# A windowed-attention block: other PSUM banks, another order of steps, and channels dealt over the partitions so that turned rows travel in single transfers

## The chip, the core and the metric

The kernel runs on one core of a Trainium2 chip. The core has a matrix engine (TensorE, PE in the profile; its weight loads are PEld), a vector engine (DVE), a scalar engine (ACT), a general engine (POOL) and an engine that issues DMA transfers (SP). They run side by side and meet at semaphores. The metric is the device time of one execution in microseconds; less is better.

## What is computed

A shifted-window transformer block over an image batch x of 4 x 256 x 256 x 96 in fp32: windows of 8 x 8 tokens, three heads of 32 channels, and an MLP of 384.

```
xs = roll(x, (-4, -4)); win = windows of 8x8 tokens of xs     # (n, 64, 96)
h = layernorm(win) * g1 + b1
q, k, v = h @ wq + bq, h @ wk + bk, h @ wv + bv               # 3 heads x 32
attn = softmax(q @ k.T / sqrt(32)); o = attn @ v
win = win + o @ wo + bo
h2 = layernorm(win) * g2 + b2
win = win + gelu(h2 @ w1 + b1) @ w2 + b2
out = roll(windows back to image, (4, 4))
```

## The kernel before, in words

**Units and batches.** A unit is half a row of windows: 16 windows, 1024 tokens, in an SBUF tile `stream` of 128 partitions x 8 tiles x 96 channels. There are 256 units in 16 batches. A batch first runs 16 attention steps, then the MLP of its 16 units. The order on each engine is written out by hand; engines wait for each other through counting semaphores.

**An attention step** works on three units at once: `back` = u, `middle` = u + 1, `front` = u + 2. PE does the scores of middle (L641), three transposes of the probabilities of back (L655), two of four q/k projections of front (L608), attention times v of back (L670), the other two projections, the v projection of front in two halves (L625), and the output projection of back in two halves (L684). DVE takes maxima of the scores (L1012), subtracts them (L1019), sums the exponentials (L1027), inverts the sums (L1035), adds the output projection into `stream` (L1041, twice) and takes statistics (L958). ACT copies out of PSUM (L806 transposed probabilities, L796/L800 q and k, L823 the attention output oT, L811 v), does the exponentials (L817) and copies the upper part of the turned, normalised input of the unit after front, `hT_upper` (L788, two halves). POOL scales the probabilities by the inverse sums (L385, three operations), makes `hT_lower` = whole minus upper (L393, two halves), and carries the arithmetic of the layer norms (L406 to L434, with the power at L425). PSUM has eight banks, and a matmul that reuses a bank has to wait until the former content has been copied out. The first half of v and the second half of the output projection share bank 6, so the second L684 waits for ACT's copy of v.

**Turned rows.** The projections want channels on the partitions. DVE transposes blocks of 32 x 32 (L1005 for the first layer norm, h1; L1072 for the second, h2), SP sends the result to a DRAM scratch tensor and fetches it back in the other order. For h2 that is three transfers of 4 x 32 x 256 elements out (L282) and one of 96 x 1024 back (L288). For h1 it is one of 128 x 3 x 256 out (L300) and three of 32 x 4 x 256 back (L310). In the MLP stretch `raw_late` (the tiles `h_raw_odd` and `oT`) takes the fetched h2 rows.

**An MLP unit.** PE runs three matmuls for each of three chunks of w1 in two parts (L718, `up`), ACT the gelus (L860), PE the second product (L732, `down`), DVE adds into `stream` (L1041). Three units ahead DVE normalises and turns (L1055, L1062, L1072), SP sends and fetches, ACT copies the upper part (L869), DVE and POOL make the lower part (L1079, L475). POOL adds b2 (L482), and does statistics for two units in the odd steps and for four units at once in steps 2 and 6. ACT also normalises the next batch's units (L777, `normalise1`, eight operations), DVE turns them. SP interleaves sends, fetches and the stores of finished units (L276: two transfers for a left half, six for a right half).

**What sets the order.** Each engine and SP's queue work in program order. A wait at the head holds all that stands behind it.

## Time and profile before

| | |
|---|---|
| median of three runs | 5499.32 us (5499.07 to 5499.84) |
| profiled execution | 5499.27 us, of which the span from first to last instruction is 5495.1 us |
| busy share of the span | PE 88%, PEld 73%, DVE 73%, ACT 72%, POOL 69% |
| mean granted TensorE clock | 0.976 of full speed |
| DMA | 622.24 MB, 113 GB/s over the span; 37.9% of 16 engines |

A busy share is a mean over stretches of different kind, so it says little alone. The profile's other views are: sums of waits (who waited for whom), a timeline for an engine (start, length, line, output and inputs, and in brackets the idle time before it and what ended it), and busy time by windows.

### The profile page before, as it was taken

How to read it: one execution, taken by the hardware profiler on the slowest of the kernel's cores; microseconds unless marked ns; L12 is line 12 of the kernel's file. 1: busy time of each engine (PE TensorE's matmuls, PEld its weight loads, DVE VectorE, ACT ScalarE, POOL GpSimd, SP SyncE). 2: the span in 40 equal slices, each digit the busy share in tenths (PEclk: the TensorE clock that was granted, in tenths of full speed). 3: DMA queues.
4: the chain of work that ended last, by engine and by line, in shares of the span. 5: the costliest groups of instructions: out<-in, count | busy, mean ns of one | idle time of the engine just before them, and what ended most of it. 6: DMA issues, size and time to landing. Idle time of an engine off the chain costs nothing.

```text
span 5495.1 us, 291417 instructions
## 1 busy us (share of the span) xinstructions
PE 4849.6 (88%) x109308; PEld 4009.3 (73%) x109308; DVE 4037.0 (73%) x9010; ACT 3956.6 (72%) x8309; POOL 3805.3 (69%) x4329
## 2 busy tenths in 40 slices
PE   6898889899898888988989888898988989888888
PEld 4777777777777777777777777777777777777777
DVE  7868768687686876868767687776877768677686
ACT  6877667686676767768677686776867677676776
POOL 6767757677575876757767577675776757767576
PEclk9999999999999999999999999999999999999999
DMA  4353433434334243343433434234342343523334
GB/s 122 112 149 95 121 104 96 145 90 122 104 99 139 89 131 102 104 132 93 133 93 112 127 92 141 87 111 126 91 144 88 114 121 89 151 88 115 112 93 148
DMA packets 443044, 622.24 MB, mean 113 GB/s; under 512 B 46009, under 2 KB 352538, under 8 KB 442586
## 3 DMA queue, kind: packets, MB, share of 16 engines
q1 hardware_dynamic: 441024, 617.92, 37.9%
q14 instruction: 449, 3.68, 0.2%
q10 hardware_dynamic: 1562, 0.50, 0.0%
q8 instruction: 9, 0.15, 0.0%
HBM read 309.96 MB, written 308.28 MB: 113 GB/s over the span
## 4 chain that ended last, share of the span: by engine, by line
PE 23%; DVE 20%; issue 17%; ACT 17%; DMA 9%; SPq 6%; POOL 5%; ACTq 2%; DVEq 1%; POOLq 0%
PE psum L732 8%; DVE row_max L1012 5%; DMA turned_rows<-probs 4%; PE psum L684 4%; ACT hT_upper L788 4%; DVE stats L958 3%; SPq L276 3%; PE psum L718 3%; DMA oT<-turned_rows 3%; PE psum L655 3%; POOL rstd L425 2%; DVE probs L1019 2%; DVE normed L1055 2%; PE psum L608 2%; PE psum L641 2%
## 5 line engine op out<-in xcount | busy, mean ns | idle before, releaser
L385 POOL TENSOR_TENSOR probs<-probs,prob_inv 128x512 f32<-128x512 f32 x771 | 782.7, 1044 | 1042.0 <-DVE prob_inv L1035 1042.0
L1041 DVE TENSOR_TENSOR stream<-stream,psum 128x384 f32 (+1 forms) x1024 | 551.3, 549 | 783.9 <-PE psum L684 484.8
L777 ACT ACTIVATE normed<-stream,shift,rstd 128x96 f32 (+1 forms) x2176 | 809.4, 462 | 76.5 <-POOL shift L434 43.0
L806 ACT ACTIVATE gelu_odd<-psum 128x512 f32<-128x512 f32 x768 | 403.5, 597 | 553.5 <-PE psum L655 553.4
L425 POOL TENSOR_TENSOR rstd<-variance,minus_half 128x16 f32<-128x16 f32 (+2 forms) x249 | 781.5, 3138 | 20.2
L684 PE MATMUL psum<-wo_w,oT 128*64 128x96 f32 x8192 | 460.4, 256 | 337.4 <-ACT v L811 337.2
L958 DVE BATCH_NORM_STATS2 stats<-stream 128x6 f32 (+2 forms) x4224 | 716.8, 243 | 42.2 <-DVE stream L1041 20.4
L684 PEld LDWEIGHTS psum<-wo_w,oT 128*64 128x64 f32 x8192 | 362.6, 139 | 422.7 <-ACT v L811 385.5
L732 PE MATMUL psum<-w_w,gelu_odd 128*64 128x96 f32 x12288 | 566.9, 255 | 112.8 <-ACT gelu_odd L860 112.7
L732 PEld LDWEIGHTS psum<-w_w,gelu_odd 128*64 128x64 f32 x12288 | 543.1, 143 | 162.7 <-issue 162.7
L732 PEld LDWEIGHTS psum<-w_w,gelu_even 128*64 128x64 f32 x12288 | 535.6, 142 | 125.5 <-issue 125.5
L732 PE MATMUL psum<-w_w,gelu_even 128*64 128x96 f32 x12288 | 559.4, 253 | 74.9 <-ACT gelu_even L860 74.4
L1019 DVE TENSOR_TENSOR probs<-psum,row_max 128x512 f32<-128x512 f32 x771 | 533.0, 691 | 26.6
L1012 DVE TENSOR_REDUCE row_max<-psum 128x8 f32<-128x512 f32 x771 | 520.6, 675 | 16.4 <-PE psum L641 16.4
L1027 DVE TENSOR_REDUCE prob_sum<-probs 128x8 f32<-128x512 f32 x771 | 488.5, 677 | 44.7 <-ACT probs L817 41.6
L817 ACT ACTIVATE probs<-probs 128x512 f32<-128x512 f32 x771 | 470.2, 625 | 65.5 <-DVE probs L1019 61.6
L482 POOL TENSOR_TENSOR stream<-stream,b_all 128x768 f32 (+1 forms) x256 | 498.2, 1949 | 18.9 <-POOL rstd L425 13.8
L860 ACT ACTIVATE gelu_odd<-psum 128x512 f32<-128x512 f32 x768 | 407.2, 587 | 94.8 <-PE psum L718 86.6
L608 PE MATMUL psum<-hT_upper,qk_split_upper 128*96 128x512 f32 x1032 | 448.2, 434 | 22.3 <-POOL hT_lower L393 22.3
L475 POOL TENSOR_TENSOR h2T_odd_lower<-oT,h2T_odd_upper 96x512 fp32r<-96x512 f32 x112 | 146.1, 1305 | 434.8 <-ACT h2T_odd_upper L869 434.8
L860 ACT ACTIVATE gelu_even<-psum 128x512 f32<-128x512 f32 x768 | 406.2, 588 | 37.4 <-PE psum L718 28.0
L608 PE MATMUL psum<-hT_lower,qk_split_upper 128*96 128x512 f32 x1032 | 409.2, 397 | 0.0
(99 smaller groups left out, 11078.6 us busy)
## 6 DMA issues: line engine op xcount, KB each, us to landing
turned_rows<-probs SPq DMA_DIRECT2D x624, 128.0 KB
turned_rows<-probs SPq DMA_DIRECT2D x208, 384.0 KB, 2.8
stream<-in_x SPq DMA_DIRECT2D x272, 192.0 KB, 3.1
h_raw_even<-turned_rows SPq DMA_DIRECT2D x390, 128.0 KB
h_raw_odd<-turned_rows SPq DMA_DIRECT2D x387, 128.0 KB
out<-stream SPq DMA_DIRECT2D x256, 192.0 KB
stream<-in_x SPq DMA_DIRECT2D x272, 180.0 KB
out<-stream SPq DMA_DIRECT2D x256, 180.0 KB
```

The source lines that it names most:

```text
L385: nc.gpsimd.tensor_tensor(block_h, block_h, inv, ALU.mult).then_inc(probs_ready, 1)
L425: nc.gpsimd.tensor_tensor(flat(rstd), variance[:, 0:n], minus_half[:, 0:n], ALU.pow)\
L482: nc.gpsimd.tensor_tensor(now, now, b2_all[:, :].unsqueeze(1).to_broadcast((P, TILES, C)), ALU.add).then_inc(b2_added, 1)
L608: last = nc.tensor.matmul(psum[0:C, QK_BANKS[n], :], qk_split[w][:, which, :], hT_split[h][:, group * SHARES:(group + 1) * SHARES], start= ...
L684: last = nc.tensor.matmul(psum[WT * side:WT * (side + 1), O_BANKS[g], t * C:(t + 1) * C], oT[:, c * P + WT * side:c * P + WT * (side + 1)] ...
L732: last = nc.tensor.matmul(psum[WT * side:WT * (side + 1), DOWN_BANKS[part], t * C:(t + 1) * C], gelu[parity][:, j, c * P + WT * side:c * P ...
L777: last = nc.scalar.activation(normed1[:, t, :], stream[:, slot, t * C:(t + 1) * C], ACT.Identity, bias=shift1[:, index, t:t + 1], scale=rs ...
L860: nc.scalar.activation(in_rows[:, 2 * part:2 * part + 2, :, :], psum[:, UP_BANKS[part][j], :].rearrange("p (b t i) -> p b t i", b=2, i=BLOCK),
L958: last = nc.vector.bn_stats(stats[:, index, c, :], stream[:, slot, c * C:(c + 1) * C])
L1012: nc.vector.tensor_reduce(row_max[:, h, :], psum[:, S_BANKS[h], :].rearrange("p (t k) -> p t k", k=WT), AXIS.X, ALU.max).then_inc(max_step, 1)
L1019: nc.vector.tensor_tensor(probs[:, buffer, h, :, :], psum[:, S_BANKS[h], :].rearrange("p (t k) -> p t k", k=WT), row_max[:, h, :].unsqueez ...
L1041: nc.vector.tensor_tensor(part, part, psum[:, banks[g], 0:GROUP], ALU.add).then_inc(added, 1)
```

## The change

It has five parts.

1. The scratch tensors in DRAM hold a turned unit as 128 partitions x 768. Every send is one transfer of 128 x 768, every fetch one of 96 x 4 x 256. The fetched channel order is then dealt over the partitions: channel 32b + c stands in partition 3c + b. The host reorders the rows of the weights that contract over channels to match (`_CHANNEL_ROWS`).
2. Banks: v in (5, 6), the output projection in (2, 3). The waits on PE move accordingly: the output projection no longer waits for v, scores wait for the first copy of v, the attention product for both, the transposes for the additions into `stream`.
3. The attention step on ACT and POOL: each exponential is moved up, the two halves of `hT_upper` and `hT_lower` are taken apart and the first stands further ahead.
4. The MLP on ACT and DVE: both gelu groups come first, then half of `normalise1`, the copy of the h2 rows, the other half; on DVE the first addition stands ahead of the lower half.
5. SP in the MLP: the fetch of h2 stands ahead of three of the six stores and of the send of h1.

```diff
-        turned_dram = nc.dram_tensor("turned_rows", (RING, CBLOCKS, BLOCK, TBLOCKS, RUN), FP32, kind="Internal").ap()
+        turned_dram = nc.dram_tensor("turned_rows", (RING, P, SEG), FP32, kind="Internal").ap()
...
-        V_BANKS = (6, 5)
-        O_BANKS = (3, 6)
+        V_BANKS = (5, 6)
+        O_BANKS = (2, 3)
...
+            def channel_major(rows):
+                return rows.rearrange("(t c) (b x) -> (c b) t x", c=BLOCK, b=CBLOCKS)
...
-                for cb in range(CBLOCKS):
-                    sp.dma_start(turned_dram[place, cb].rearrange("c t x -> t c x"),
-                                 source[:, RUN * cb:RUN * (cb + 1)]).then_inc(h2_left, 16)
+                sp.dma_start(turned_dram[place], source).then_inc(h2_left, 16)
...
-                sp.dma_start(raw, turned_dram[place].rearrange("b c t x -> (b c) (t x)"))\
+                sp.dma_start(raw.rearrange("q (t x) -> q t x", t=TBLOCKS), channel_major(turned_dram[place]))\
...
-                    store(batch_row + i // 2, i % 2)
+                    store(batch_row + i // 2, i % 2, slice(0, 3))
+                    fetch_late(batch + i + 4, n)
+                    if i % 2:
+                        store(batch_row + i // 2, 1, slice(3, 6))
                     if i >= 2:
                         send_h1(batch + BATCH + i + 1, turned1_late)
-                    fetch_late(batch + i + 4, n)
...
+                    copy_hT_lower(batch + s + 3, (s + 3) % 2, 0)
                     normalise_probs(batch + s + 1, (s + 1) % 2)
-                    copy_hT_lower(batch + s + 3, (s + 3) % 2)
+                    copy_hT_lower(batch + s + 3, (s + 3) % 2, 1)
...
-                need(v_copied, 2 * (u + 1))
+                need(v_copied, 2 * u + 1)
...
-                wait_apart(pe, attn_added, 2 * u + 2)
+                wait_apart(pe, v_copied, 2 * (u + 2))
...
                 if g == 0:
+                    wait_apart(pe, qk_copied, 4 * (u + 2) + 2)
                     pe.wait_ge(oT_copied, 2 * (u + 1))
-                else:
-                    pe.wait_ge(v_copied, 2 * (u + 2) + 1)
...
+                def mlp_step(j, odd, norm):
                     gelus(batch + j, odd, 1)
+                    gelus(batch + j + 1, 1 - odd, 0)
+                    if norm:
+                        normalise1(batch + BATCH + j + 1, j + 1, range(TILES // 2))
                     copy_h2T_upper(batch + j + 2, odd)
-                    gelus(batch + j + 1, 1 - odd, 0)
+                    if norm:
+                        normalise1(batch + BATCH + j + 1, j + 1, range(TILES // 2, TILES))
...
+                    add_mlp(batch + j, 0)
                     copy_h2T_lower(b, j + 2, parity)
-                    add_mlp(batch + j)
+                    add_mlp(batch + j, 1)
```

**PE at the end of an attention step**, first as before and then as changed: the v projection of front (L625, then L627), the output projection of back (L684, then L686) and the scores of the next step (L641, then L643).

```order
L625 MATMUL psum<-qkv_w,h_raw_odd 32x96 [waits oT_copied,h1_back_odd]
L625 MATMUL psum<-qkv_w,h_raw_odd 32x96 x15
L589 REGISTER_ALU
L625 MATMUL psum<-qkv_w,h_raw_odd 32x96 [waits shift_done]
L625 MATMUL psum<-qkv_w,h_raw_odd 32x96 x15
L684 MATMUL psum<-wo_w,oT 64x96 [waits oT_copied]
L684 MATMUL psum<-wo_w,oT 64x96 x7
L684 MATMUL psum<-wo_w,oT 64x96 [waits v_copied]
L684 MATMUL psum<-wo_w,oT 64x96 x7
```

```order
L627 MATMUL psum<-qkv_w,h_raw_odd 32x96 [waits shift_done]
L627 MATMUL psum<-qkv_w,h_raw_odd 32x96 x15
L627 MATMUL psum<-qkv_w,h_raw_odd 32x96 [waits oT_copied]
L627 MATMUL psum<-qkv_w,h_raw_odd 32x96 x15
...
L686 MATMUL psum<-wo_w,oT 64x96 [waits qk_copied,oT_copied]
L686 MATMUL psum<-wo_w,oT 64x96 x15
```

The second half of the output projection has no wait of its own any more, and the two waits of the v projection have changed places.

**ACT in an attention step**, before and changed: `gelu_odd` is where the transposed probabilities go, L817 (then L821) are the exponentials, L788 (then L792) the copy of `hT_upper`, L811 (then L815) that of v.

```order
L806 ACTIVATE gelu_odd<-psum 128x512 x3
L796 ACTIVATE qT<-psum 96x128x4
L800 ACTIVATE kT<-psum 96x16x32
L817 ACTIVATE probs<-probs 128x512
L823 ACTIVATE oT<-psum 96x8x16x4 x2
L817 ACTIVATE probs<-probs 128x512 x2
L796 ACTIVATE qT<-psum 96x128x4
L800 ACTIVATE kT<-psum 96x16x32
L788 ACTIVATE hT_upper<-h_raw_odd 96x512 x2
L811 ACTIVATE v<-psum 128x384 x2
```

```order
L810 ACTIVATE gelu_odd<-psum 128x512 x3
L821 ACTIVATE probs<-probs 128x512
L800 ACTIVATE qT<-psum 96x128x4
L804 ACTIVATE kT<-psum 96x16x32
L821 ACTIVATE probs<-probs 128x512
L827 ACTIVATE oT<-psum 96x8x16x4 x2
L821 ACTIVATE probs<-probs 128x512
L792 ACTIVATE hT_upper<-h_raw_even 96x512
L800 ACTIVATE qT<-psum 96x128x4
L804 ACTIVATE kT<-psum 96x16x32
L815 ACTIVATE v<-psum 128x384 x2
L792 ACTIVATE hT_upper<-h_raw_even 96x512
```

The first half of `hT_upper` has moved ahead of the second qT and kT, the second half behind v.

**SP in the MLP**, one odd unit, before and changed: L282 (then L284) sends h2, L276 are stores, L300 (then L301) sends h1, L288 (then L289) fetches h2.

```order
L282 DMA turned_rows<-probs 4x32x256 x3
L276 DMA out<-stream 15x4x768
L276 DMA out<-stream 4x384 x2
L276 DMA out<-stream 15x4x768
L276 DMA out<-stream 4x384 x2
L300 DMA turned_rows<-probs 128x3x256
L288 DMA oT<-turned_rows 96x1024
```

```order
L284 DMA turned_rows<-probs 128x768
L276 DMA out<-stream 15x4x768
L276 DMA out<-stream 4x384 x2
L289 DMA oT<-turned_rows 96x4x256
L276 DMA out<-stream 15x4x768
L276 DMA out<-stream 4x384 x2
L301 DMA turned_rows<-probs 128x768
```

The send is one transfer, and the fetch has moved ahead of three stores and of the send of h1.

## Rows read from the trace of the kernel before

**Rows 1.** Windows: stretch, length, busy of PE, PEld, DVE, ACT, POOL, clock, DMA share.

```profile
1420.10:1603.50 183.40, 161.52 (x4978) 129.46 (x4978) 143.33 (x342) 139.34 (x280) 125.65 (x143) 0.98 0.30 89
1603.50:1761.10 157.60, 142.91 (x1841) 122.54 (x1842) 105.18 (x211) 104.71 (x231) 109.67 (x122) 0.96 0.46 137
```

**Rows 2.** Sums of waits: engine and line, releaser: us in total, times, longest.

```profile
ACT h2T_odd_upper L869 <- DMA oT<-turned_rows: 366.1, 107, 7.6
...
PE psum L684 <- ACT v L811: 337.2, 255, 6.0
...
ACT h2T_even_upper L869 <- DMA h_raw_odd<-turned_rows: 209.5, 81, 4.8
```

**Rows 3.** Timeline of PE, one attention step: start, length, instruction, [idle before].

```profile
1516.48 1.28 PE L641 MATMUL psum<-kT,qT 32*64 32x64 f32 x96
...
1524.68 0.88 PE L684 MATMUL psum<-wo_w,oT 128*64 128x96 f32 x16
1526.33 0.88 PE L684 MATMUL psum<-wo_w,oT 128*64 128x96 f32 x16 [0.76 <-ACT v L811]
1527.14 1.29 PE L641 MATMUL psum<-kT,qT 32*64 32x64 f32 x96
```

**Rows 4.** Timeline of ACT, the same step.

```profile
1522.75 1.14 ACT L817 ACTIVATE probs<-probs 128x512 f32<-128x512 f32 x2
...
1525.78 0.87 ACT L811 ACTIVATE v<-psum 128x384 f32<-128x384 f32 x2
```

**Rows 5.** Timeline of DVE, the same step.

```profile
1516.64 0.55 DVE L1041 TENSOR_TENSOR stream<-stream,psum 128x384 f32 x1 [1.01 <-PE psum L684]
1517.34 1.38 DVE L958 BATCH_NORM_STATS2 stats<-stream 128x6 f32 x8 [0.15 <-DVE stream L1041]
...
1524.72 0.30 DVE L1035 RECIPROCAL prob_inv<-prob_sum 128x24 f32<-128x24 f32 x1
```

**Rows 6.** Timeline of POOL, the same step; a two-unit call runs from L406 on.

```profile
1519.86 0.24 POOL L406 TENSOR_TENSOR mean_gap<-stats 128x16 f32<-128x16 f32 x1
...
1521.78 2.91 POOL L425 TENSOR_TENSOR rstd<-variance,minus_half 128x16 f32<-128x16 f32 x1
1525.10 3.05 POOL L385 TENSOR_TENSOR probs<-probs,prob_inv 128x512 f32<-128x512 f32 x3 [0.41 <-DVE prob_inv L1035]
1528.11 2.53 POOL L393 TENSOR_TENSOR hT_lower<-h_raw_odd,hT_upper 96x512 fp32r<-96x512 f32 x2
```

**Rows 7.** Timeline of SP's queue, start of an MLP stretch.

```profile
1615.48 1.84 SPq L282 DMA_DIRECT2D turned_rows<-probs  x3
1621.97 0.32 SPq L288 DMA_DIRECT2D oT<-turned_rows  x1
```

**Rows 8.** Windows (a send; after a PE wait), and the landings of L300.

```profile
1617.50:1621.50 4.00, 4.00 (x51) 3.33 (x53) 2.49 (x4) 0.45 (x1) 0.00 (x0) 1.00 0.26 89
1659.50:1666.30 6.80, 5.63 (x70) 5.63 (x72) 3.38 (x11) 6.08 (x16) 4.96 (x11) 0.50 0.66 196
...
DMA to landing us min/median/max: 2.5/2.9/6.1
```

**Rows 9.** Timelines of POOL, ACT and PE in the MLP stretch.

```profile
1637.77 1.01 POOL L406 TENSOR_TENSOR mean_gap<-stats 128x32 f32<-128x32 f32 x1
...
1641.45 5.44 POOL L425 TENSOR_TENSOR rstd<-variance,minus_half 128x32 f32<-128x32 f32 x1
...
1656.13 2.97 ACT L777 ACTIVATE normed<-stream,shift,rstd 128x96 f32 x8 [1.36 <-POOL shift L434]
...
1660.67 6.91 PE L732 MATMUL psum<-w_w,gelu_odd 128*64 128x96 f32 x96 [3.33 <-ACT gelu_odd L860]
...
1671.82 4.18 PE L732 MATMUL psum<-w_w,gelu_even 128*64 128x96 f32 x96
...
1680.23 4.18 PE L732 MATMUL psum<-w_w,gelu_odd 128*64 128x96 f32 x96
```

**Rows 10.** Timeline of ACT, the opening step of a batch.

```profile
1433.61 1.15 ACT L788 ACTIVATE hT_upper<-h_raw_odd 96x512 fp32r<-96x512 f32 x2 [5.14 <-DMA h_raw_odd<-turned_rows]
```

More of the change, by code:

```diff
@@ L768, in absent, with normalise1, copy_hT_upper @@
                 return isinstance(u, int) and u < 0
[L770 to L774 removed]
+            def normalise1(u, index, tiles=range(TILES)):
+                if tiles[0] == 0:
+                    wait_apart(act, rstd1_ready, u + 1)
+                    if not (isinstance(u, int) and u == 0):
+                        wait_apart(act, h1_turned, u)
                 slot = u % SLOTS if isinstance(u, int) else u & (SLOTS - 1)
[L776 removed]
+                for t in tiles:
                     last = nc.scalar.activation(normed1[:, t, :], stream[:, slot, t * C:(t + 1) * C], ACT.Identity,
                                                 bias=shift1[:, index, t:t + 1], scale=rstd1[:, index, t:t + 1])
[L779 to L789 removed]
+                if tiles[-1] == TILES - 1:
+                    last.then_inc(ln1_ready, 1)
+            def copy_hT_upper(u, parity, g):
+                if g == 0:
+                    wait_apart(act, h1_back[parity], 8 * (u - parity) + 16)
+                if not (isinstance(u, int) and u == 0):
+                    act.wait_ge(qk_done, 4 * (u - 1) + 2 * g + 2)
+                tokens = slice(g * SHARES, (g + 1) * SHARES)
+                nc.scalar.activation(hT_split[0][0:C, tokens], h_raw[parity][0:C, tokens], ACT.Copy)\
+                    .then_inc(hT_upper_copied, 1)
             def copy_qk(u, n):
@@ L834, in attention_step @@
                         copy_probsT(back, h)
+                if not absent(middle):
+                    exps(middle, 1 - half, 0)
                 if not absent(front):
@@ L838, in attention_step @@
                 if not absent(middle):
-                    exps(middle, 1 - half, 0)
+                    exps(middle, 1 - half, 1)
                 if not absent(back):
@@ L843, in attention_step @@
                 if not absent(middle):
-                    exps(middle, 1 - half, 1)
                     exps(middle, 1 - half, 2)
+                copy_hT_upper(u + 3, 1 - half, 0)
                 if not absent(front):
@@ L848, in attention_step @@
                     copy_qk(front, 3)
-                copy_hT_upper(u + 3, 1 - half)
-                if not absent(front):
                     copy_v(front, half, 0)
                     copy_v(front, half, 1)
+                copy_hT_upper(u + 3, 1 - half, 1)
             def gelus(u, parity, part):
@@ L920, in mlp @@
                 for j in (0, 1):
-                    mlp_step(j, j)
+                    mlp_step(j, j, False)
                 with act.Fori(1, BATCH // 2 - 1) as k:
                     for odd in (0, 1):
-                        j = 2 * k + odd
-                        mlp_step(j, odd)
-                        normalise1(batch + BATCH + j + 1, j + 1)
+                        mlp_step(2 * k + odd, odd, True)
                 gelus(batch + BATCH - 2, 0, 1)
+                gelus(batch + BATCH - 1, 1, 0)
                 normalise1(batch + 2 * BATCH - 1, BATCH - 1)
-                gelus(batch + BATCH - 1, 1, 0)
                 gelus(batch + BATCH - 1, 1, 1)
@@ L1080, in copy_h2T_lower, with add_mlp @@
                                         h2T[parity][0][0:C, first], ALU.subtract).then_inc(h2T_ready[0], 1)
[L1082 to L1086 removed]
+            def add_mlp(u, g):
+                if g == 0:
+                    dve.wait_ge(b2_added, u + 1)
+                dve.wait_ge(down_done, 2 * u + g + 1)
+                add_into_stream(u, DOWN_BANKS, g, mlp_added)
             def attention_step(u, half):
```

84 lines of the change are left out of this document (34 added, 50 removed).

## The prediction

> **What bounds the kernel now.** I read the two kinds of stretch apart first. One batch of 16 units takes about 341 us: 183.4 in attention and 157.6 in the MLP [rows 1]. TensorE is busy 161.5 and 142.9 of these, the other engines 105 to 143, so PE sets the pace, and what can be won is its waiting and its slow clock, not the other engines' idle time. The sums of waits then say where PE and its feeders stand [rows 2]: PE waits 337.2 us for the copy of v before L684, 21 us a batch, and in the MLP ACT, which feeds it, waits 366.1 + 209.5 us for rows that come back by DMA.
>
> **Attention step by step.** From scores (L641) to the first L684 is 8.20 us without a gap; the second L684 then waits 0.76 and starts 1.65 after the first; scores follow 0.81 later, and the step is 10.66 [rows 3]. The first block of L684 is 0.88 busy, of which about 0.78 is its pitch, so PE's own floor is 8.20 + 0.81 + 0.81, with rounding 9.85. Why is v late? The second L684 ends, DVE adds (1516.64), does its statistics, and goes through maxima and shifts; ACT does its last exponentials at 1522.75, then qT, kT and both halves of hT_upper (1.15, as in [rows 10]), and v only at 1525.78 [rows 4, 5]; PE may go on at 1526.33. This is a closed ring of about 10.65 us: L684, add, statistics, shifts, exp, qT and kT, hT_upper, v, L684. Everything that DVE does more after a step (first statistics 1.4, a transpose 0.95) lengthens it; such steps take up to 11.5.
>
> **The change in attention.** (a) The banks: the output projection uses banks 2 and 3 and no longer waits for v; the next scores wait for the first v copy only. The ring is cut, which by itself frees the waits of 15 steps, the 21 us a batch less the opening step's 6. (b) What is late next: in the new order ACT copies the first half of hT_upper behind the third exp, POOL subtracts the first lower half (half of 2.53, 1.27) and only then scales the probabilities (3.05) that the next step's transposes need [rows 6]. The new ring, by ACT's pitches (about 0.5 an operation, since two exps take 1.14 with their overlap [rows 4]; the last of a row is seen 0.05 later): from the last transpose, 0.63 to its end and semaphore, copy 0.52, exp 0.54, qT and kT 1.08, exp 0.55, two oT 1.0, exp 0.54, hT_upper 0.57, lower 1.27, probabilities 3.05, hand-over 0.2: 9.95 us, as long as PE's 9.85. So plain steps come to 9.95. (c) DVE's extra pieces stand in nine steps, POOL's extra pieces in eleven (for two units a call of 5.0: 4.83 from L406 to the end of the power, and one small operation [rows 6]): a POOL step with a call is 5 + 2.53 + 3.05 = 10.6 to 10.8, about 0.7 over. A late start is given back in part by the next step, because the ring through DVE and POOL goes over two steps; I let a piece of 1.45 cost 0.75 a step, one of 0.95 cost 0.45, a POOL call 0.6 where no DVE piece covers it, and ACT's three normalise1 blocks (2.97 [rows 9], against 1.9 of slack) 0.5 each beyond that: 2.2 + 2.7 + 1.2 + 1.5 = 7.6. PE's added instructions for separate waits (two a step) I cannot price from a row; nothing to 0.1 us each, taken at 0.05: 1.5 a batch, half of it hidden behind the ring in (b): 0.8. Steps 2 to 15: before 15 waits of about 1.05 plus what they carried, 16.5 us over the floor in the traced batch; after 0.1 x 14 + 7.6 + 0.8 = 9.8 less about 1 that falls together. That is 7.7 won.
> (d) The opening step: ACT waits 5.14 us at hT_upper for h_raw_odd [rows 10], whose fetch SP issues when the last stores have landed. One transfer in place of three saves two issues, some 0.9 us. But hT_upper's first half now stands ahead of the last qT and kT and of v, and on POOL ahead of the probabilities: all of them wait there. PE has then done both L684 and waits in front of scores: 1434.8 against 1436.66, 1.9 won; the cold clock behind it stays. With 0.5 in the second step, attention gives 10 us a batch (from 4, if rings (b) and (c) cost double, to 14, if they are hidden).
>
> **The change in the MLP.** A unit is 8.41 us of PE between two L732 blocks [rows 9]; 16 are 134.6 and the opening and closing pieces add some 2.4, so that 137.0 is the floor and 20.6 of the 157.6 are lost. Where: a turned unit goes out at 1615.48 in three transfers and its fetch is issued at 1621.97, 6.5 us later [rows 7]. Of these 1.84 are issue. In between the DMA share is 0.26 [rows 8]: four of sixteen engines' worth, and the outermost dimension of each transfer counts four. The send of h1, the same 384 KB with 128 partitions outermost, takes 2.9 us to land [rows 8]. The new send has 128 partitions outermost and one piece of 3 KB in each: I take 2.9, with 2.5 and 6.1 (the row's ends) as bounds. The fetch changes from 96 runs of 4 KB to 384 of 1 KB; the nearest row is that same one, whose 384 runs were 1 KB on both sides, so I take no loss, up to 1 us as bound. So the rows are back about 3.6 us sooner; SP's split of the six stores puts the fetch ahead of three of them, and send_h1 no longer stands ahead of it. ACT's copy of the rows is now behind the next gelus and half of a normalise1: 1.5 + 1.4 later, but those gelus no longer wait for a DMA. The rows land some 5 us before their copy is due, and the DMA waits leave PE's path.
> The Trainium skill (DMA: Bandwidth & Descriptors, Why a DMA increments its semaphore by 16 and not by 1) says that a transfer is spread over the largest number up to 16 that divides the slowest dimension of both sides; the trace agrees with 0.26 for a dimension of four. By that rule the new send and fetch (128 and 96) use all sixteen. If instead the bytes set the landing, as one might read the 6.5 us, the MLP would keep almost none of its gain, which is rival C.
>
> **What stays in the MLP.** POOL's four-unit statistics (5.44 for the power, 9.1 from L406 to its end) end late, the next call of 5 behind them later still; ACT's normalise1 waits for it until 1656.13, the second gelus of that unit stand behind it, and PE waits 3.33 at 1660.67 [rows 9], after which its clock is 0.50, the 1.2 GHz level, for 6.8 us [rows 8]. In the new order the chain starts 3.5 us sooner (POOL gets the rows sooner), but the copy of the next rows now stands inside normalise1: 1.1 more ahead of the gelus. Laid out from the first L732: POOL's lower half of unit 4 at 22.1 to 23.4, the long call to 32.5, b2 and a lower half to 35.6, the call of 5 to 40.6, half of normalise1, the copy, the other half to 44.6, gelus to 46.2; PE wants them at 42.05. That is 4.2 of waiting and 1.7 of clock; the second long call by the same steps 3.3 and 1.7; 1.5 for all the rest: 12.4, or 13.3 with 0.9 for DVE operations that POOL holds up. So 7.3 won of 20.6 (from 2, if the landing is at its upper bound, to 14, if POOL's calls are hidden).
>
> **Sum.** 10 + 7.3 = 17.3 a batch, times 15 = 260. In the first batch ACT has a normalise1 (2.97) in every step on top of some 8.15 of other work (139.3 of [rows 1], less three normalise1, over 16 steps): 11.1 with its hand-overs nearly the step itself, so I give its attention 1 and its MLP 5. Together 266. The profiled execution took 5499.27 (span 5495.1 and 4.2 around it), the median is 5499.32: 5233, rounded 5235 us.
>
> **Rivals.** A: the new ring in attention is a little longer than I sum, and gives all back. It needs 0.7 us a step, less than one POOL operation; what speaks for it is that 9.95 has no slack, against it that inv is ready at 1525.0 [rows 5] and POOL waited for it. Only the MLP gains: 5499 - 7.3 x 15 - 5 = 5385.
> B: POOL's long calls stall PE far less, since all that feeds them is sooner, and the clock stays up: 6 more a batch, 5235 - 96 = 5140.
> C: the single send lands no sooner than the three did. The MLP keeps 1.3 a batch (the issues), attention its 10: 5499 - 11.3 x 15 - 1 = 5330. A and C together: 5480.
> D, slower: ACT's copy of the rows stands behind a normalise1 that waits for POOL, and POOL's next call stands behind the lower half that waits for this copy. Ring: call 5.0, half a normalise1 1.5, copy 1.1, two lower halves 2.5, two b2 3.7: 13.8 in every two units, against PE's 16.8. It turns the result round when it takes more than 16.8 + 17.3/7 = 19.3 in all seven pairs; at 20 it would be 5235 + 3.2 x 7 x 16 = 5593. No row of POOL is stretched that far.
>
> **Chances.** Forecast 0.60 (its own range 5170 to 5300), A 0.14, B 0.10, C 0.09, A with C 0.03, D 0.04. The range 5130 to 5390 takes in the forecast, A, B and C with their bounds, and leaves out under 0.2. About 0.2%, 11 us, is what a measurement of this kernel tells from no change: faster 0.94, within 0.02 (the joint case, a little worse), slower 0.04.
>
> **What would show it.** Right: no wait of PE for v before the second L684; plain attention steps of 9.9 to 10.1; a send that lands in about 3 us with the DMA share near 1 while it runs; ACT's 576 us of waits for returned rows gone for the most part; a PE wait of some 4 us left behind each of the two long POOL calls, with the clock at 0.50 after it. Wrong: PE waiting 0.7 or more before the transposes of most steps for POOL's probabilities (A); no PE wait over 2 us in the MLP (B); a share of 0.26 during the send (C); ACT waiting for POOL's shift in every other MLP unit (D).

## The result: no gain, where 5% was forecast

| | before | changed |
|---|---|---|
| median of 20 runs | 5499.19 us (5492.04 to 5506.98) | 5506.94 us (5500.80 to 5516.28) |
| span of the profiled execution | 5495.1 us | 5498.5 us |
| mean granted TensorE clock | 0.976 | 0.965 |
| DMA packets | 443044 | 374339 |

The ratio is 1.0015, with a 95% interval of 1.0008 to 1.0021: 0.15% slower, within 0.2% of no change. The forecast was 5235, with a range of 5130 to 5390.

The page of the changed kernel shows busy shares as before; in its chain of work that ended last POOL has 21%, where it had 5% before, 8% in the power of the statistics (L424) alone, and ACT's `normalise1` (L780) and DVE's L1062 stand there too.

```profile
PE 4914.6 (89%) x109308; PEld 3995.0 (73%) x109308; DVE 4067.4 (74%) x9010; ACT 3932.1 (72%) x8309; POOL 3782.6 (69%) x4329
...
PE 25%; POOL 21%; issue 19%; DVE 14%; ACT 11%; DMA 5%; ACTq 2%; SPq 2%; DVEq 2%; POOLq 1%
POOL rstd L424 8%; PE psum L610 6%; POOL probs L385 4%; DVE normed L1062 4%; PE psum L734 4%; PE psum L720 3%; DMA h_raw_odd<-turned_rows 3%; PE psum L627 3%; ACT normed L780 3%; PE psum L686 2%; PE psum L658 2%; PE psum L673 2%; DVE stream L1048 2%; DVE stats L965 2%; DVE normed L1069 2%
```

**The two stretches of one batch.** From here on a batch is cut at PE: attention runs from the first scores (L641, now L643) to the first second product of the MLP (L732, now L734), the MLP from there to the next scores. The windows of batch 4, before (first fence) and changed (second), with the columns of [rows 1]:

```profile
1420.10:1610.90 190.80, 168.69 (x5021) 135.13 (x5021) 149.48 (x353) 145.87 (x290) 133.05 (x148) 0.98 0.29 87
1610.90:1761.10 150.20, 135.73 (x1799) 116.87 (x1799) 99.03 (x201) 98.19 (x221) 102.27 (x117) 0.95 0.47 142
```

```profile
1424.30:1608.20 183.90, 169.33 (x5019) 134.07 (x5019) 149.51 (x353) 142.54 (x289) 132.65 (x148) 0.97 0.31 91
1608.20:1764.40 156.20, 135.66 (x1798) 114.47 (x1797) 100.68 (x201) 99.92 (x222) 100.33 (x117) 0.97 0.41 137
```

Attention is 6.9 us shorter, the MLP 6.0 longer. The means over the fifteen batches after the first say the same: attention 189.3 to 182.7, MLP 149.7 to 155.8. So the change did act: 6.6 us a batch were won in attention, and 6.1 were lost again in the MLP.

**The waits.** The sums of waits of the changed kernel, with the columns of [rows 2]:

```profile
ACT normed L780 <- POOL shift L433: 467.6, 97, 7.3
...
DVE h2T_even_lower L1086 <- ACT h2T_even_upper L874: 405.4, 96, 6.9
...
PE psum L720 <- DVE h2T_even_lower L1086: 251.1, 80, 5.2
...
ACT normed L780 <- DVE probs L1012: 191.0, 80, 3.5
...
ACT hT_upper L792 <- DMA h_raw_odd<-turned_rows: 140.8, 57, 8.4
...
PE psum L643 <- ACT v L815: 135.5, 67, 7.8
```

The 337.2 us of PE in front of L684 [rows 2] have left no row; what PE still waits for v is 135.5 us in front of scores, 104.4 of it in the opening steps of fourteen batches. ACT's waits for fetched h2 rows, 366.1 and 209.5 us [rows 2], are gone. In their place ACT waits 467.6 us for POOL and 191.0 for DVE at `normalise1`, and PE waits 251.1 for the rows whose copy stands behind it.

**The send.** The row on the send's line (L284) and the windows at a send issued at 1611.51, where [rows 8] had a share of 0.26:

```profile
DMA to landing us min/median/max: 2.3/2.4/3.2
```

```profile
1612.40:1613.40 1.00, 1.00 (x5) 0.82 (x6) 1.00 (x4) 0.07 (x1) 0.81 (x1) 1.00 0.94 372
```

It lands in 2.4 us and keeps nearly all sixteen DMA engines busy.

**A plain attention step** of PE, against [rows 3]:

```profile
1454.21 1.29 PE L643 MATMUL psum<-kT,qT 32*64 32x64 f32 x96
...
1458.45 1.20 PE L673 MATMUL psum<-gelu_odd,v 64*32 64x64 f32 x96
...
1462.60 1.54 PE L686 MATMUL psum<-wo_w,oT 128*64 128x96 f32 x32
1464.07 1.29 PE L643 MATMUL psum<-kT,qT 32*64 32x64 f32 x96
```

From scores to scores it is 9.86 us in place of 10.66, and the output projection is one piece without a wait.

**The MLP stretch.** The timelines of ACT, DVE, POOL and PE from the wait of unit 5 to that of unit 7 (PE's L720 makes `up`, L734 the second product; ACT's L874 copies the h2 rows):

```profile
1649.72 1.54 ACT L780 ACTIVATE normed<-stream,shift,rstd 128x96 f32 x4 [7.08 <-POOL shift L433]
1651.17 1.13 ACT L874 ACTIVATE h2T_even_upper<-h_raw_odd 96x512 fp32r<-96x512 f32 x2
...
1660.28 1.55 ACT L780 ACTIVATE normed<-stream,shift,rstd 128x96 f32 x4 [3.07 <-DVE probs L1012]
1661.73 1.14 ACT L874 ACTIVATE h2T_odd_upper<-oT 96x512 fp32r<-96x512 f32 x2
...
1671.45 1.54 ACT L780 ACTIVATE normed<-stream,shift,rstd 128x96 f32 x4 [4.27 <-POOL shift L433]
1672.90 1.13 ACT L874 ACTIVATE h2T_even_upper<-h_raw_odd 96x512 fp32r<-96x512 f32 x2
```

```profile
1651.81 0.69 DVE L1086 TENSOR_TENSOR h2T_even_lower<-h_raw_odd,h2T_even_upper 96x512 fp32r<-96x512 f32 x1 [6.57 <-ACT h2T_even_upper L874]
1652.42 0.54 DVE L1048 TENSOR_TENSOR stream<-stream,psum 128x384 f32 x1
1652.88 3.46 DVE L1062 TENSOR_TENSOR normed<-stream,mean 128x768 f32 x1
...
1658.95 0.94 DVE L1012 STREAM_TRANSPOSE probs<-normed 128x768 f32<-128x768 f32 x1
```

```profile
1663.05 1.28 POOL L474 TENSOR_TENSOR h2T_odd_lower<-oT,h2T_odd_upper 96x512 fp32r<-96x512 f32 x1 [7.52 <-ACT h2T_odd_upper L874]
1664.29 0.95 POOL L405 TENSOR_TENSOR mean_gap<-stats 128x16 f32<-128x16 f32 x1
...
1670.69 0.22 POOL L433 TENSOR_TENSOR shift<-minus_mean,rstd 128x16 f32<-128x16 f32 x1
```

```profile
1652.74 0.76 PE L720 MATMUL psum<-h2T_even_upper,w_split_upper 128*128 128x512 f32 x1 [4.43 <-DVE h2T_even_lower L1086]
1653.30 0.63 PE L720 MATMUL psum<-h2T_even_upper,w_split_lower 128*128 128x512 f32 x1
...
1674.48 0.47 PE L720 MATMUL psum<-h2T_even_upper,w_split_upper 128*128 128x512 f32 x1 [2.16 <-DVE h2T_even_lower L1086]
```

The rows for the copy at 1651.17 had been in SBUF for long: they were fetched at 1637.74, and the landings of L289 take 3.1 to 5.2 us. What held the copy was its place in ACT's order, behind a half `normalise1` that could start only when POOL's shift came. The copy sets off DVE and through it PE. Behind it DVE works off its order in a row and ends L1012 at 1659.9; the next half `normalise1` has waited for that, the next copy stands behind it, POOL has stood 7.52 us for this copy and only then begins its next call, for which the next `normalise1` waits. From copy to copy these are 10.56 and 11.17 us (1651.17, 1661.73, 1672.90), and PE needs 8.41 for a unit. Copies go on at this pace: in this batch the pairs of units from 1651.17 on take 21.7, 22.8, 21.5 and 21.6 us from copy to copy, against 16.8 of PE. A matmul of L720 takes 0.63 after the wait, where 0.39 is usual; the granted clock from 1652.7 to 1656.5 is 0.56.

**The opening step**: ACT waits longer than the 5.14 us of [rows 10], and PE with it.

```profile
1439.69 0.63 ACT L792 ACTIVATE hT_upper<-h_raw_odd 96x512 fp32r<-96x512 f32 x1 [8.25 <-DMA h_raw_odd<-turned_rows]
```

```profile
1441.90 2.04 PE L643 MATMUL psum<-kT,qT 32*64 32x64 f32 x96 [7.67 <-ACT v L815]
```

### The profile page after: what moved, and what is told of

It is laid out like the page before. It is cut to its first block, busy times and chain, and to the rows that moved or that the text cites. A ratio compares the mean times of both kernels' runs of the same rounds, so it can differ in the third digit from the quotient of the medians.

```text
span 5498.5 us, 289773 instructions
## 1 busy us (share of the span) xinstructions
PE 4914.6 (89%) x109308; PEld 3995.0 (73%) x109308; DVE 4067.4 (74%) x9010; ACT 3932.1 (72%) x8309; POOL 3782.6 (69%) x4329
## 2 busy tenths in 40 slices
DMA packets 374339, 622.21 MB, mean 113 GB/s; under 512 B 38745, under 2 KB 240826, under 8 KB 373882
## 4 chain that ended last, share of the span: by engine, by line
PE 25%; POOL 21%; issue 19%; DVE 14%; ACT 11%; DMA 5%; ACTq 2%; SPq 2%; DVEq 2%; POOLq 1%
POOL rstd L424 8%; PE psum L610 6%; POOL probs L385 4%; DVE normed L1062 4%; PE psum L734 4%; PE psum L720 3%; DMA h_raw_odd<-turned_rows 3%; PE psum L627 3%; ACT normed L780 3%; PE psum L686 2%; PE psum L658 2%; PE psum L673 2%; DVE stream L1048 2%; DVE stats L965 2%; DVE normed L1069 2%
## 5 line engine op out<-in xcount | busy, mean ns | idle before, releaser
L780 ACT ACTIVATE normed<-stream,shift,rstd 128x96 f32 (+1 forms) x2176 | 828.1, 459 | 662.4 <-POOL shift L433 467.6
L392 POOL TENSOR_TENSOR hT_lower<-h_raw_odd,hT_upper 96x512 fp32r<-96x512 f32 x258 | 329.3, 1276 | 679.5 <-ACT hT_upper L792 675.6
L424 POOL TENSOR_TENSOR rstd<-variance,minus_half 128x16 f32<-128x16 f32 (+2 forms) x249 | 762.8, 3064 | 20.3
L810 ACT ACTIVATE gelu_odd<-psum 128x512 f32<-128x512 f32 x768 | 422.5, 597 | 440.5 <-PE psum L658 435.2
L734 PEld LDWEIGHTS psum<-w_w,gelu_odd 128*64 128x64 f32 x12288 | 528.8, 141 | 80.1 <-issue 80.1
L720 PE MATMUL psum<-h2T_even_upper,w_split_upper 128*128 128x512 f32 x768 | 352.0, 458 | 252.6 <-DVE h2T_even_lower L1086 251.1
L734 PE MATMUL psum<-w_w,gelu_odd 128*64 128x96 f32 x12288 | 552.6, 251 | 19.7 <-ACT gelu_odd L865 19.7
L821 ACT ACTIVATE probs<-probs 128x512 f32<-128x512 f32 x771 | 487.2, 632 | 94.8 <-DVE probs L1026 94.7
L734 PEld LDWEIGHTS psum<-w_w,gelu_even 128*64 128x64 f32 x12288 | 511.3, 137 | 57.3 <-issue 57.3
L734 PE MATMUL psum<-w_w,gelu_even 128*64 128x96 f32 x12288 | 535.2, 247 | 9.3 <-ACT gelu_even L865 8.0
L392 POOL TENSOR_TENSOR hT_lower<-h_raw_even,hT_upper 96x512 fp32r<-96x512 f32 x260 | 332.4, 1279 | 288.1 <-ACT hT_upper L792 287.2
L658 PE MATMUL psum<-ident,probs 128*128 128x128 f32 x3072 | 466.6, 290 | 70.8 <-POOL probs L385 50.9
L643 PE MATMUL psum<-kT,qT 32*64 32x64 f32 x24672 | 349.6, 230 | 152.4 <-ACT v L815 135.5
L865 ACT ACTIVATE gelu_odd<-psum 128x512 f32<-128x512 f32 x768 | 415.8, 587 | 96.9 <-PE psum L720 78.7
```

What stands on the lines that cost most here:

```text
L392: nc.gpsimd.tensor_tensor(lower[:, tokens], h_raw[parity][0:C, tokens], upper[:, tokens], ALU.subtract).then_inc(hT_copied, 1)
L424: nc.gpsimd.tensor_tensor(flat(rstd), variance[:, 0:n], minus_half[:, 0:n], ALU.pow)\
L658: last = nc.tensor.transpose(psum[:, PT_BANKS[h], quad * P:(quad + 1) * P], probs[:, buffer, h, 2 * quad:2 * quad + 2, :].rearrange("p a k ...
L720: last = nc.tensor.matmul(psum[:, UP_BANKS[part][j], :], w1_split[w][:, j * P:(j + 1) * P], h2T[parity][h][:, part * SHARES:(part + 1) * S ...
L734: last = nc.tensor.matmul(psum[WT * side:WT * (side + 1), DOWN_BANKS[part], t * C:(t + 1) * C], gelu[parity][:, j, c * P + WT * side:c * P ...
L780: last = nc.scalar.activation(normed1[:, t, :], stream[:, slot, t * C:(t + 1) * C], ACT.Identity, bias=shift1[:, index, t:t + 1], scale=rs ...
```

## The experiments

The kernel before was timed again beside each group of runs: its median was 5500.65 us beside the first four, 5506.26 beside the next four and 5502.86 beside the last two, and 5499.19 beside the changed kernel. A difference of times between two groups is therefore known to some 7 us only, and every ratio is to the kernel before of its own group. First the change was taken apart. ACT's order in the MLP cannot be changed alone: its copy would wait for a fetch that SP issues behind a send of h1, which waits for that `normalise1`. So parts 4 and 5 go together.

**Part 1 alone**, the kernel before with the new scratch layout and single transfers:

```diff
-                for cb in range(CBLOCKS):
-                    sp.dma_start(turned_dram[place, cb].rearrange("c t x -> t c x"),
-                                 source[:, RUN * cb:RUN * (cb + 1)]).then_inc(h2_left, 16)
+                sp.dma_start(turned_dram[place], source).then_inc(h2_left, 16)
```

> The kernel before with the single transfers (part 1) alone. Theory N (in the changed kernel the half of normalise1 that stands ahead of the copy of the h2 rows makes ACT wait for POOL's statistics while the rows have long landed, and this eats what the transfers give): here the copy still stands first, so the sooner rows pay. The stall before the third L732 of a batch (3.5 us) and some 3 us of the later ones go, about 6 us a batch: 5400 us. Rival P (POOL's two long calls set the MLP's length, whatever order ACT has): under 1 us a batch, 5485 us or more. If the opening step depends on where SP's loop head lies in the code, the first interval between scores may be anything between 15 and 18 us here too.

Measured: 5416.72 us, ratio 0.9847 (0.9830 to 0.9863). The transfers are worth 84 us. The MLP falls from 149.7 to 142.4 us a batch, but attention rises from 189.3 to 191.6, of which 1.6 are the opening step (16.0 to 17.6).

**Parts 2 and 3 alone**, banks and attention order:

```diff
-        V_BANKS = (6, 5)
-        O_BANKS = (3, 6)
+        V_BANKS = (5, 6)
+        O_BANKS = (2, 3)
```

(and the order of ACT, POOL and PE in an attention step, as in the change)

> The kernel before with banks and attention order (parts 2 and 3) alone, its 3 + 3 transfers and its MLP kept. From the changed kernel's trace the steps 2 to 15 win 7.5 us a batch. The opening step should win about 1 (v no longer held to the end), since SP's code is that of before: 5499 - 8.5 x 15 = 5370 us. Against it, if the attention gain were tied to the single transfers (h1 landing sooner), steps 2 to 15 would stay over 10.6 us and the time over 5450 us.

Measured: 5357.07 us, ratio 0.9733 (0.9717 to 0.9749). Worth 144 us; attention is 180.0, the MLP 150.1.

**Parts 4 and 5 alone**, the MLP order of ACT, DVE and SP:

```diff
-                def mlp_step(j, odd):
+                def mlp_step(j, odd, norm):
                     gelus(batch + j, odd, 1)
+                    gelus(batch + j + 1, 1 - odd, 0)
+                    if norm:
+                        normalise1(batch + BATCH + j + 1, j + 1, range(TILES // 2))
                     copy_h2T_upper(batch + j + 2, odd)
-                    gelus(batch + j + 1, 1 - odd, 0)
+                    if norm:
+                        normalise1(batch + BATCH + j + 1, j + 1, range(TILES // 2, TILES))
```

> The kernel before with the MLP order of ACT, DVE and SP (parts 4 and 5) alone; the attention order and the three transfers per send are those of before. Theory N: the MLP gets longer, as in the changed kernel, by 5 to 8 us a batch (waits of ACT at normalise1 for POOL's shift with the copy behind them), 5580 to 5630 us. Rival P: within 1 us a batch, 5485 to 5515 us.

Measured: 5722.1 us, ratio 1.0406 (1.0388 to 1.0423). It costs 221 us, more than was expected; the MLP is 162.9 a batch. Both kinds of wait at `normalise1` are there with the old transfers too:

```profile
ACT normed L780 <- DVE probs L1011: 467.5, 141, 5.9
...
ACT normed L780 <- POOL shift L436: 317.1, 52, 7.2
PE psum L720 <- DVE h2T_even_lower L1085: 299.6, 96, 5.1
```

**Parts 1 to 3 together**, the changed kernel with the MLP order of before (the reverse of the diff above):

> The changed kernel with the MLP order of before (parts 1 to 3 kept, 4 and 5 undone). Theory N: both gains stay, some 6 in attention and 6 in the MLP a batch: 5310 us. Rival P: only attention's, 5400 us. Rival X (single transfers themselves harm the MLP, by packets of 1 KB or by collisions with loads and stores): 5450 us or more.

Measured: 5274.19 us, ratio 0.9590 (0.9574 to 0.9606). The parts add: 84 + 144 = 228 expected from the single runs, 226 measured. What parts 4 and 5 cost on top is 5507 - 5274 = 233 us, about as much as they cost alone (221). The loss is in the MLP order, and it eats the whole gain.

**Which line of the order?** The changed kernel with ACT's copy ahead of the whole of `normalise1`; DVE's and SP's new order stay.

```diff
                     gelus(batch + j + 1, 1 - odd, 0)
-                    if norm:
-                        normalise1(batch + BATCH + j + 1, j + 1, range(TILES // 2))
                     copy_h2T_upper(batch + j + 2, odd)
                     if norm:
-                        normalise1(batch + BATCH + j + 1, j + 1, range(TILES // 2, TILES))
+                        normalise1(batch + BATCH + j + 1, j + 1)
```

> The changed kernel with one thing undone on ACT in the MLP: the copy of the h2 rows stands ahead of normalise1 again, which is whole behind it; both gelu groups stay ahead of the copy, and SP's and DVE's new order stay. Theory N (it is normalise1's wait for POOL with the copy behind it): the MLP falls to that of the run without part 4 and 5, about 142 us a batch, so 5270 to 5290 us. Rival G (the gelus ahead of the copy, or DVE's addition ahead of the lower half, or SP's order, cost it): 5400 us or more.

Measured: 5269.74 us, ratio 0.9570 (0.9554 to 0.9586). The place of one copy is worth 237 us (245 by the two ratios). The timelines of ACT, POOL and PE at the unit that stalled:

```profile
1585.69 1.14 ACT L874 ACTIVATE h2T_even_upper<-h_raw_odd 96x512 fp32r<-96x512 f32 x2
1593.15 2.97 ACT L780 ACTIVATE normed<-stream,shift,rstd 128x96 f32 x8 [6.32 <-POOL shift L433]
...
1598.89 1.15 ACT L874 ACTIVATE h2T_odd_upper<-oT 96x512 fp32r<-96x512 f32 x2
```

```profile
1600.22 1.27 POOL L474 TENSOR_TENSOR h2T_odd_lower<-oT,h2T_odd_upper 96x512 fp32r<-96x512 f32 x1 [2.85 <-ACT h2T_odd_upper L874]
```

```profile
1597.70 5.83 PE L734 MATMUL psum<-w_w,gelu_odd 128*64 128x96 f32 x96 [4.12 <-ACT gelu_odd L865]
```

ACT waits for POOL nearly as long as in the changed kernel (6.32 us, 7.08 there), but the copy is done, and PE has run all eighteen matmuls of L720 by 1593.6. PE then waits 4.12 for the gelus and has a slow L734 (5.83, where 4.18 is usual); the second long call gives 3.16 and 5.83; and no unit behind them stalls. The MLP is 141.15 a batch.

**Is POOL's long call what remains?** Parts 1 to 3, with the statistics of two units in each of four calls:

```diff
-                    if j in (2, 6):
-                        at = 8 + (j - 2)
-                        finish2(call, batch + at, at, LN_GROUP)
+                    if j in (2, 4, 6, 8):
+                        at = 6 + j
+                        finish2(call, batch + at, at, 2)
```

> Parts 1 to 3 with the old MLP order (5274 us), and POOL's two statistics calls over four units in the MLP made into four calls over two, in steps 2, 4, 6 and 8. Theory C (a long call holds the next two-unit call, for which ACT's normalise1 and the gelus behind it wait): the two intervals of 12.4 and 12.0 us between L732 blocks fall to under 9.5, 5 to 7 us a batch with the clock: 5180 us. Rival: POOL's sum of work or the port it shares with DVE decides, then the stalls are spread over more units and the time is 5260 or more.

Measured: 5280.89 us, ratio 0.9590 (0.9574 to 0.9607), no better than unsplit (5274.19, the same ratio). Theory C was wrong and its rival came true: the stalls moved and were not removed. The two units that took 12.5 and 11.9 us now take 11.2 and 9.3, but two that took 8.4 take 8.9 and 11.8. The sum of ACT's waits for POOL even rose from 99.9 us to

```profile
ACT normed L777 <- POOL shift L431: 259.7, 71, 5.8
```

and POOL's timeline there has no wait over 0.5 us for 64 us (1576 to 1640): this speaks for the sum of its work in these units being late, and not one long call. Whether fewer or cheaper operations on POOL would remove it was not tried.

**The opening step.** SP's queue, from the last send to the fetch of the first h1 rows, before, changed, and in the run with both repairs (below). The batch's first scores on PE are at 1420.09, 1424.29 and 1360.05.

```profile
1415.24 9.59 SPq L276 DMA_DIRECT2D out<-stream  x8
1429.59 1.36 SPq L310 DMA_DIRECT2D h_raw_odd<-turned_rows  x3
```

```profile
1419.49 9.62 SPq L276 DMA_DIRECT2D out<-stream  x8
1435.65 0.36 SPq L309 DMA_DIRECT2D h_raw_odd<-turned_rows  x1
```

```profile
1355.18 9.65 SPq L276 DMA_DIRECT2D out<-stream  x8
1369.41 0.36 SPq L309 DMA_DIRECT2D h_raw_odd<-turned_rows  x1
```

Behind the first scores the fetch goes out after 9.50, 11.36 and 9.36 us. SP's instructions in the trace say where this time goes. In every version SP is past its wait for the stores 5.9 us behind the scores, and then stands still for 2.5 to 2.8 us at the turn of its batch loop. In the changed kernel it stands still for another 2.1 us after the loop's first instruction (8.69 to 10.79 behind the scores); before the change it does not. Code comes in as packets of 8 KB on a DMA queue of its own (q14, "instruction", in the list of queues), and one such packet runs in the middle of this stop. If the place of the loop's head among these pieces is the cause, moving the code by a few instructions should end the stop. Two idle instructions ahead of the loop:

```diff
+            for _ in range(2):
+                sp.sem_inc(passed, 1)
             with sp.Fori(1, BATCHES) as b:
```

> The changed kernel with two idle semaphore instructions on SP ahead of its batch loop, nothing else. In the changed kernel's trace SP stands still for 2.2 us behind the first instruction of the loop, once a batch, while an 8 KB piece of instructions comes in. Theory H (the loop head lies across two such pieces): the stop goes, the first interval of a batch falls from 17.4 to about 15.3 us, and the time by 2.1 x 15 = 31 us, to 5475 us. Rival: the landing of the stores or the fetch sets it, 5507 us and the stop stays.

Measured: 5489.19 us, ratio 0.9971 (0.9959 to 0.9982). The stop is gone, and the first interval falls from 17.4 to 15.5 us, as expected, but only 18 us of the expected 31 are kept (24 by the two ratios); in the traces the MLP takes 0.7 a batch back. In the kernel of parts 1 to 3 alone the stop is 1.6 us and stands a few instructions later; eight idle instructions there:

> Parts 1 to 3 with the old MLP order and eight idle semaphore instructions on SP ahead of its batch loop, so that the loop head lies early in an instruction piece. Theory H: 1.8 us a batch, 5274 - 27 = 5247 us, and the first interval 15.1 instead of 16.9. Rival: 5274 us.

Measured: 5252.15 us, ratio 0.9533 (0.9516 to 0.9551): 22 us won (31 by the two ratios), and the first interval falls from 16.9 to 15.8.

**Both repairs in the changed kernel**, the copy ahead and the two idle instructions:

> The changed kernel with both repairs: ACT's copy of the h2 rows ahead of the whole normalise1 (the MLP order of the run that gave 5269.74), and two idle instructions on SP ahead of its batch loop. The theory is that the two causes are independent, one in the MLP, one at the start of the attention stretch, so that their savings add: the loop head gave 17.7 us in the changed kernel and 22.0 in the one with the MLP order of before. Expected 5250 us (5246 to 5254), ratio 0.954; first attention interval 15.5 in place of 17.4. The rival is that the MLP takes back what the opening step gives, since SP and POOL come to it in another phase: 5265 to 5270, no gain over the copy ahead alone.

Measured: 5246.06 us, ratio 0.9538 (0.9522 to 0.9554). They add, as far as the noise lets one say: 5269.74 - 5246.06 = 23.7 us (18 by the two ratios), first interval 15.5, where the rival had no gain. With the run before it this is the best version found, and the intervals of the two do not tell them apart.

**The copy between the gelus**, with the same two idle instructions:

```diff
                     gelus(batch + j, odd, 1)
-                    gelus(batch + j + 1, 1 - odd, 0)
                     copy_h2T_upper(batch + j + 2, odd)
+                    gelus(batch + j + 1, 1 - odd, 0)
```

(with all of `normalise1` behind them)

> As the kernel with both repairs, but ACT's copy of the h2 rows stands between the two gelu groups, where it stands in the kernel before, and all of normalise1 behind both; DVE's and SP's MLP order stay those of the changed kernel. If only the place relative to normalise1 matters (the theory: head of line behind a normalise1 that waits for POOL), this is the same time as with the copy behind both gelu groups, 5245 to 5260. The rival: the copy, 1.1 us of ACT in front of the second gelu group, or the wait for the fetch, again stands in PE's path as it does in the kernel before; since the fetch is issued before its three late stores it should land in time, but if not, ACT's waits for the DMA return (over 100 us in all) and the time is 5280 or more.

Measured: 5267.18 us, ratio 0.9574 (0.9558 to 0.9590), between the two expectations. The MLP is 142.4 a batch against 140.9 with the copy behind both gelus. ACT waits 68 and 74 us for fetched rows, a quarter of what it did before the change:

```profile
ACT h2T_odd_upper L876 <- DMA oT<-turned_rows: 74.0, 33, 3.6
...
ACT h2T_even_upper L876 <- DMA h_raw_odd<-turned_rows: 68.2, 63, 1.6
```

So the place relative to `normalise1` makes the large difference, 237 us, and the place relative to the gelus a small one, 21 us. Given the new order of DVE and SP, putting both gelus first was right. Against the whole order of before the intervals show no gain from parts 4 and 5 even with the copy moved: with the stop on SP repaired, the old order took 5252.15 and the new one with both gelus and the copy ahead 5246.06. The run of this section has ACT's order of before, and stands 15 us above that 5252.15 with DVE's and SP's orders of before too; what in these two orders costs it was not taken apart.

## Why the prediction was wrong

**Where the 266 us went.** By batch, the forecast was 10 us won in attention and 7.3 in the MLP; measured are 6.6 won and 6.1 lost. Attention misses 3.4 a batch, 51 us in fifteen; the MLP 13.4, 201 us, and 17 more in the first batch (144.7 to 156.3, where 5 were to be won). The reading of the bottleneck was right, and so were two of the three mechanisms: the banks, which take the wait for v away, and the single transfers. The third, the new place of ACT's copy in the MLP, was wrong, and it alone turned the result round. That the time came out so near to no change is a chance meeting of 226 us won and 233 lost.

**Attention, steps 2 to 15: right.** Forecast 7.7 won. Measured between the third and the last scores 144.2 to 136.9, and 0.4 in the last step: 7.7. No wait for v is left before L686, and plain steps take 9.86 us where 9.95 was expected. So POOL's probabilities, moved behind half of `hT_lower`, do not set the step (PE waits for them 50.9 us in the whole run), and rival A falls. The total of 7.7 is met; its single terms for DVE's and POOL's extra pieces were not measured one by one, so how far errors in them cancel stays open.

**Attention, the opening step: wrong, 3.3 us a batch.** The step was: one transfer in place of three saves two issues, 0.9, and hT_upper ahead of v is worth 1.0 more. Measured is 1.35 lost (16.01 to 17.36). Two things stood against it. A single fetch lands 4.0 us after its issue,

```profile
DMA to landing us min/median/max: 3.3/4.0/4.8
```

and the three of before, issued over 1.36 us, had their rows usable 4.0 after the first issue (1429.59 to 1433.61 of [rows 10]), so the saved issues had not been on the path. Over the opening steps of the later batches the medians from first issue to use are 3.75 before and 3.92 changed. And SP stopped for 2.1 us just ahead of this fetch. The prediction also had the fetch wait for the landing of the last stores; in the traces SP is past that at 5.9 us, and the turn of its loop, which no term of the sum held, takes another 2.5 to 2.8. The reordering was worth something by itself: with parts 2 and 3 alone the interval is 15.2, 0.8 less than before.

**The send and fetch: right.** 2.4 us to land where 2.9 was taken; ACT's 576 us of waits for returned rows are down to about 1. By the Trainium skill (DMA: Bandwidth & Descriptors, Why a DMA increments its semaphore by 16 and not by 1) a transfer with 128 as its slowest dimension uses all sixteen engines; the trace agrees, with 0.94 where a slowest dimension of four had 0.26. Rival C falls. Part 1 alone won 7.3 us a batch in the MLP, and together with the copy behind both gelus and ahead of `normalise1` 8.55 (149.7 to 141.15).

**ACT's copy inside `normalise1`: the step that failed.** The prediction put the copy "1.5 + 1.4 later", which is the work of the gelus and of half a `normalise1`, and priced it as 1.1 us of ACT in front of the gelus of a late unit, which is the copy's own length. The wait that stands in front of this half `normalise1`, 7.08 us for POOL at 1649.72 and 467.6 in the whole run, was put at nothing for the copy. The copy now shares it. Three readers stand behind it: PE's L720 of the unit after, DVE's whole order through L1086, and POOL's next call through L474. The sum followed the gelus to PE and none of these three. The units of the MLP, from one L734 to the next, as medians over the last fifteen batches, with 8.41 as the floor of each:

| stretch | forecast | changed | copy ahead |
|---|---|---|---|
| at the first long call (two intervals) | 5.9 over | 7.3 over | 6.2 over |
| at the second long call (two intervals) | 5.0 over | 7.7 over | 4.9 over |
| all the rest | 2.4 over | 11.4 over | 0.5 over |
| sum | 13.3 | 26.3 | 11.5 |

The waits behind the two long calls were sized well, for a kernel whose copy does not stand behind them: 4.2 and 3.3 forecast, 4.12 and 3.16 in the run with the copy ahead, each with 1.65 of slow clock. The term of the sum in which the missing wait shows is "1.5 for all the rest", with the 0.9: 11.4 us were measured. These are above all the excesses of 2.8, 2.8, 1.9 and 3.2 us in later units, to one of which the PE wait at 1674.48 shown above belongs.

**Rival D was the case, with a leg missing.** It named the copy behind a `normalise1` that waits for POOL, and the ring through POOL's next call. It took the ring as 13.8 us in two units against PE's 16.8, so that it would never decide, and gave it 0.04. The ring read from the trace is 21.7 in two units (1651.17 to 1672.90). It does not hold PE from the first unit on: the first four intervals of a batch are at the floor. So the loss is smaller than the 5593 that D named for a ring of 20 in all seven pairs. What the sum lacked: in every other unit the half `normalise1` waits not for POOL but for DVE's L1012, which stands behind four operations and L1086, which waits for the copy. From copy to copy this leg is 10.56 us. The other leg, through POOL, is 11.2: call 6.6 in place of 5.0, since two of its small operations (L405, shown above, and L407) take 0.95 in place of 0.23. Without the stretched operations (L1062 2.5 us shorter, the call 1.6) an estimate of the ring is still 17.6, over PE's 16.8; no run had it so. The prediction's own list of what would show it wrong had the right line, "ACT waiting for POOL's shift in every other MLP unit (D)": 97 waits, 467.6 us.

**What would have told.** [rows 9] showed `normalise1` ready at 1656.13 behind POOL, and the third L732 from there at 1680.23. Every operation moved behind that wait should have had its readers' due times written beside it. For the rows of the next unit that is its first L720: PE had done all before it at 1648.3 in the changed kernel, when POOL's shift was not yet out (L433 at 1648.95 in its timeline), and the copy is a half `normalise1` of 1.5 us behind that.

## What to carry to other kernels

On an engine that works in order, an operation moved behind one that waits for another engine inherits that wait, and so do all readers of its result; price it by those readers' due times, not by its own length. When two such operations feed each other through two other engines, write out the ring with every leg, operations of the in-between engine included, and compare it with the pace of the bottleneck. When a change has parts in different stretches, look at each stretch by itself first: here 226 us were won and 233 lost, and the total showed neither.

## What the runs showed of the hardware

- **Where the head of SP's loop lies.** The place of the loop's head in the instruction stream changes the time: two idle instructions in front of it took 18 us off the changed kernel and 24 off the one with the copy ahead (5506.94 to 5489.19, and 5269.74 to 5246.06; 24 and 18 by the ratios), eight took 22 off another version, over fifteen passes of the loop. That the stop is the loading of a piece of 8 KB is inferred. For it speaks that the two idle instructions take fourteen pieces away from the whole run, about one in each pass. It is not shown: in the stop itself runs one q14 packet (9.18 us behind the scores), and the repaired kernel has a packet at the same place (9.27) without a stop; and the kernel before loads 449 pieces with no such stop. The rows of that queue on the pages of the changed kernel and of the one with the two idle instructions:

```profile
q14 instruction: 448, 3.67, 0.2%
```

```profile
q14 instruction: 434, 3.56, 0.2%
```

- **Merging fetches saves issue time, not latency.** In the opening step one transfer of 96 x 4 x 256 was in use 4.0 us after its issue, as late as three of 32 x 4 x 256 after their first issue.
- **DVE beside POOL.** DVE's L1062 took 0.94 or 0.95 us in all fifteen cases in which no operation of POOL ran beside it, and also beside POOL's power (L424) in 32 cases. Beside POOL's addition of b2 it took 3.46 (1652.88 to 1656.34), and it ended 0.81 after POOL's addition did (1653.71 to 1655.53): nearly its own length, as if it had stood still until then. POOL's L405 took 0.95 in place of 0.23 when DVE's L1062 ran. Why they hold each other up was not tested. The row below has L1062 at its short length; the one operation of POOL beside it, L415, took 0.97 in place of its usual 0.20.

```profile
1621.44 0.95 DVE L1062 TENSOR_TENSOR normed<-stream,mean 128x768 f32<-128x768 f32 x1
```
